# Which engine writes the halved high tiles: from VectorE to ScalarE, from unit 6 on

## The reference, cut to what matters

```
x = x + conv(group_norm(x), w0, b0)      # then the same with w1, b1
conv(f): fn = f / |f| over the channels
         vol = for each of the 5 x 5 shifts: sum over channels of fn * shifted fn     # 25 planes
         relu(w @ concat(f, vol) + b)                                                   # w is (512, 537)
```

## Time and profile before

| | us |
|---|---|
| median of 3 runs | 499.98 |
| lowest and highest | 497.35, 500.1 |
| profiled execution, its own time | 502.14 |
| its span in the trace | 500.4 |
| TensorE busy | 438.5 (88%) |
| VectorE busy | 370.1 (74%) |
| ScalarE busy | 288.1 (58%) |
| GpSimd busy | 119.1 (24%) |

### The profile page before, as it was taken

One profiled execution on the slowest core, in us unless ns is written; L12 is line 12 of the kernel. 1 busy time (PEld: TensorE's weight loads), 2 busy tenths in 40 slices (PEclk: granted clock), 3 DMA queues, 4 the chain that ended last, 5 costly groups with the idle time before them and its releaser, 6 DMA issues.

```text
span 500.4 us, 13879 instructions
## 1 busy us (share of the span) xinstructions
PE 438.5 (88%) x5896; PEld 225.3 (45%) x5896; DVE 370.1 (74%) x871; ACT 288.1 (58%) x346; POOL 119.1 (24%) x171
## 2 busy tenths in 40 slices
PE   0356599288699999999999999999999999999996
PEld 0342345153354545444444545454545454544442
DVE  6797797786777979597869797898879797533422
ACT  1454273647359585677757484849495857623222
POOL 3505340131111313105031313131313131143100
PEclk9968889879799999999999999999999999999999
DMA  8361351623131273526758684232222325355222
GB/s 298 127 220 51 99 193 57 180 55 74 45 94 32 66 227 99 162 106 208 267 172 260 225 258 131 63 83 67 73 78 61 90 78 156 149 170 177 104 118 92
DMA packets 33988, 65.87 MB, mean 132 GB/s; under 512 B 11756, under 2 KB 21028, under 8 KB 33926
## 3 DMA queue, kind: packets, MB, share of 16 engines
q1 hardware_dynamic: 24134, 56.07, 34.1%
q0 software_dynamic: 9792, 8.92, 7.5%
HBM read 33.54 MB, written 28.87 MB: 125 GB/s over the span
## 4 chain that ended last, share of the span: by engine, by line
PE 50%; DVE 21%; DMA 11%; ACT 10%; issue 4%; SPq 2%; POOL 2%; DVEq 0%; ACTq 0%
PE conv_ps L579 39%; DVE stats L820 7%; DVE operands L867 4%; ACT operands L685 4%; PE conv_ps L588 4%; PE gram_ps L501 3%; DMA skew<-band_dram 3%; DVE xs L952 3%; ACT v L692 3%; DMA band_dram<-band 3%; DMA vol<-corr_h 2%; PE gram_ps L514 2%; SPq L369 1%; ACT act_out L721 1%; POOL v L444 1%
## 5 line engine op out<-in xcount | busy, mean ns | idle before, releaser
L579 PE MATMUL conv_ps<-operands,wh 128*128 128x512 f16 x1024 | 327.8, 382 | 0.6 <-DVE wl L940 0.6
L579 PE MATMUL conv_ps<-operands,wl 128*128 128x512 f16 x512 | 195.4, 382 | 0.0
L579 PEld LDWEIGHTS conv_ps<-operands,wh 128*128 128x128 f16 x1024 | 101.7, 99 | 119.8 <-issue 3.5
L721 ACT ACTIVATE act_out<-conv_ps,bias,wdown 128x512 f32<-128x512 f32 x128 | 95.4, 771 | 86.4 <-PE conv_ps L588 84.0
L952 DVE TENSOR_TENSOR xs<-xs,act_out 128x512 f32<-128x512 f32 x128 | 85.7, 683 | 38.6 <-ACT act_out L721 38.6
L685 ACT ACTIVATE operands<-xs,affine 128x1024 f16<-128x1024 f32 x64 | 93.1, 1460 | 19.9 <-DVE affine L860 19.9
L867 DVE TENSOR_TENSOR operands<-v,operands 128x1024 f16<-128x1024 f32 x64 | 82.4, 1288 | 25.5 <-ACT v L692 19.8
L820 DVE BATCH_NORM_STATS2 stats<-xs 128x6 f32<-128x512 f32 x128 | 79.8, 681 | 2.5 <-DMA xs<-in_x_dram 2.5
L579 PEld LDWEIGHTS conv_ps<-operands,wl 128*128 128x128 f16 x512 | 50.4, 99 | 56.2 <-issue 1.6
L692 ACT ACTIVATE v<-xs,affine 128x1024 f32<-128x1024 f32 x52 | 68.5, 1317 | 0.0
L323 POOL DMA_DIRECT2D vol<-corr_h x48 | 33.1, 697 | 119.3 <-DVE corr_h L889 119.2
(11 more groups left out here) (75 smaller groups left out, 220.2 us busy)
## 6 DMA issues: line engine op xcount, KB each, us to landing
xs<-in_x_dram SPq DMA_DIRECT2D x32, 512.0 KB, 7.3
out_dram<-xs SPq DMA_DIRECT2D x32, 512.0 KB, 3.1
band_dram<-band SPq DMA_DIRECT2D x64, 120.0 KB, 2.6
skew<-band_dram SPq DMA_DIRECT2D x32, 222.5 KB, 3.1
vol<-corr_h POOLq DMA_DIRECT2D x48, 50.0 KB, 3.3
rows_dram<-rows SPq DMA_DIRECT2D x32, 65.8 KB
rows_dram<-rows SPq DMA_DIRECT2D x32, 63.3 KB
mirror<-rows_dram POOLq DMA_DIRECT2D x14, 110.9 KB, 2.5
```

Source lines behind the costliest of these rows:

```text
L579: pe.matmul(conv_ps[:, g % 4, :], w[:, l, t, m * P:(m + 1) * P], opnd[:, u % RING, part, t, n * HALF:(n + 1) * HALF], start=(t == 0 and w ...
L721: act.activation(in_rows(act_out[:, g % AOUT, :]), by_rows(conv_ps[:, g % 4, :]), ACT.Relu, bias=bias[:, l, m:m + 1], scale=wdown[:, l, m: ...
```

## The change

For units 6 to 15 ScalarE writes the halved tile, right behind the exact tile of the same t, and VectorE's half_tile returns at once. Units 0 to 5 are as before. The new function waits for the products of the unit before (which read half) and for its own high tile. The wait of TensorE on halved is not changed.

```
         def half_on_act(u):

             return u > STEADY + 2

@@ ScalarE
             def act_half_tile(u, t):

                 if half_on_act(u):
                     act.wait_ge(gram, BANKS * u)
                     act.wait_ge(high, KT * u + t + 1)
                     act.activation(half[:, t, :], opnd[:, u % RING, 0, t, :], ACT.Copy, scale=0.5
                                    ).then_inc(halved, 1)
...
                     norm_tile(k + 1, 0)
                     exact_tile(k + 1, 0)
+                    act_half_tile(k + 1, 0)
...
                     norm_tile(k + 1, 1)
                     exact_tile(k + 1, 1)
+                    act_half_tile(k + 1, 1)
...
                     if j in (1, 2) and valid(k + 1):
                         exact_tile(k + 1, j + 1)
+                        act_half_tile(k + 1, j + 1)
@@ VectorE
             def half_tile(u, t):

+                if half_on_act(u):
+                    return
                 wait(dve, gram, BANKS * u)
                 dve.tensor_scalar(half[:, t, :], opnd[:, u % RING, 0, t, :], 0.5, None, ALU.mult).then_inc(halved, 1)
```

## The result

The changed kernel takes **514.67 us** (median; 512.21 to 515.77), the kernel before 498.76 in the same comparison. The ratio is 1.029, with a 95% interval of 1.0251 to 1.0329: slower by 15.9 us from median to median. Two of the four runs of before took 497.35 and 497.55 us, the other two 499.98 and 500.1; in larger sets, on other chips, its medians are 499.94, 500.46 and 501.25, and 514.67 is 13.4 to 14.7 us above these. The profiled execution took 513.97 us, with a span of 512.1; that is 11.8 more than the profiled execution of before (502.14). The forecast was 513.7 and +13.75.

A forecast was written before the change was run, and what follows sets the result against it. TensorE's own work was taken to bound the kernel from slot 5 on, at 26.13 us a slot. Stalls in ten slots summed to 13.75 us, which on the median of 499.98 gave 513.7 us, range 507 to 524.

The forecast's parts named there:

- The bound: From slot 5 on TensorE's own work sets the pace, with a floor of 26.13 us a slot.
- The price of the copy: Each ScalarE copy of a halved tile lasts 1.05 us and moves what is queued behind it by 0.95 us.
- The stall: TensorE waits at step 6 for step 2's rectified group: 3.8 - 0.8 - 1.5 = 1.5 us in slot 12.
- Hole and slack: Slot 12: ScalarE idles 0.8 us before the lengths; step 2's rectified group is 1.5 us ahead of TensorE's need.
- A: Theory: an awaited rectified group stands behind ScalarE's copies; every slot pays 4 x 0.95 us less a hole and a slack.
- Nothing is taken back, nothing piles up: TensorE's 8.60 us of gapless work after step 6 recovers no stall; each slot pays anew, without accumulating lateness.
- The sum: Stalls of ten slots, 5 to 14: 6.0 + 1.5 + 2.4 + 1.1 + 1.3 + 1.45 = 13.75 us.
- (a): Rival: not slower, through larger slack or a copy under 0.57 us in slot 12; 498 to 500 us, chance 0.14.
- (b): Rival: copy near the exact tile's price, or late rows copy delays TensorE through the volume; 524 us, 0.10 with (c).
- (c): Rival: stalls lower TensorE's clock, costing 2 us more a slot; 534 us, chance 0.10 together with (b).

The follow-up runs named there:

- VectorE's relief alone: Against the kernel before: from unit 6 VectorE halves only 8 of 1024 columns per tile, products read the high tile, ScalarE unchanged; 499.99 us, ratio 1.0001.
- the later unit: Against the changed kernel: halved tiles move to ScalarE from unit 11 on in place of unit 6; 506.62 us, ratio 1.0129 to the kernel before.
- The other place: Against the changed kernel: same forty copies, tile 0 before the lengths, 1 behind the last exact tile, 2 and 3 behind the rows copy; 505.17 us.
- the two halves: Two kernels against the changed one: ScalarE halves only tiles 0 and 1, or only 2 and 3, VectorE the others; 504.55 and 508.41 us.
- the half length: Against the changed kernel: ScalarE writes columns 0 to 511 of each halved tile, VectorE the other 512; 502.1 us, ratio 1.0047 to the kernel before.
- the kernel with the copies alone: Against the changed kernel: VectorE halves all tiles again, ScalarE's forty copies go into a spare buffer nobody reads; 514.54 us, ratio 1.0306 to before.

## Why the prediction was right

**The bound.** Right. TensorE's 26.13 us a slot is a floor: the kernel with VectorE's relief alone has it in most slots, and in none of the eleven kernels is a slot from 5 on shorter by more than 0.02 us.

**The price of the copy.** Taken as 1.05 us and 0.95 in the queue, measured 1045 ns and 0.94. The value lies between the line through other forms (986 ns) and the weights' scaling (1104), as reasoned. The overlap was quoted as 0.10 from rows that give 0.13 (1.34 - 1.21); the copy's own is 0.09. The sentence on the Trainium skill ("ScalarE: Activation LUTs", "What ACT_TABLE_LOAD costs") gave 1039 ns; the trace agrees with it within 6 ns. The rule of the same page of the Trainium skill that sends multiplications to VectorE ("Rules for kernel authors") also holds here: 1045 ns against 444.

**The stall.** Hole and slack were read right, and the estimate of 0.1 us for the semaphore, which no row had been given for, is 0.07 (386.68 - 386.61). 3.8 - 0.8 - 1.5 = 1.5 us was forecast for slot 12 at step 6, and the group of step 6 starts 18.98 - 17.53 = 1.45 us later in its slot. Step 5 was to be 0.2 to 0.3 late and is 0.31. That a late volume or neighbour tile would be covered by this stall was right too: slot 8 has a wait of 0.6 us for the volume and is no longer than the others. The copies into a spare buffer and the later unit come out in A's ranges (the latter with a rise of 5.4 to 6.4 us where 7.6 was given). The other place, the two halves and the half length move as the order asks and not as the load does, but each ended 1 to 4 us over A's range. Two smaller readings were off. TensorE did wait for ScalarE once from 150 us on, 0.5 us at 164 us, ahead of the slots that count. And the list of waits was to show 1.5 us a slot; it shows 0.97.

**Nothing is taken back, nothing piles up.** Right: ten waits, nine nearly equal slots, and five waits when five slots are changed. That VectorE stays just ahead of the average was right as well, with 0.05 to 0.09 us to spare. In the kernel with tiles 0 and 1 moved VectorE was later, and did become the limit.

**The sum.** Here a term was mis-sized. Slots 6 and 7 were given 1.2 us and slot 8 1.1, on top of slots of 27.56, 27.14 and 27.28 us, with waits for the skew transfer, the neighbours and the statistics taken as part of the kernel. Measured from trace to trace these slots grow by 0.23, 0.56 and 0.41 only, slots 5 and 10 to 13 by 1.48 to 1.56, slot 9 by 1.21, and the nine sum to 10.0 us. The reason is that most of those waits did not come again. In slot 6 the lengths start 212.51 - 199.81 = 12.70 us behind the average in the trace, and 11.87 in the changed kernel, where ScalarE's chain alone puts them at 11.75. Had they been as late again, the slot of 28.20 us in the kernel with the copies alone suggests that it would have cost nearly as much more. Against typical slots of before, 236.1 us for nine, the change costs 1.43 a slot, 14.3 in ten; the rule of 1.5 in each of ten would have given 15.0.

So the way the total came out is in part luck. On its own base the sum made 515.9 us, 1.9 over the profiled execution. The same 13.75, lowered by waits of one trace, was then put on a median of executions that mostly don't have these waits, and that gave 513.7, 1.0 under the measured median. The rise from median to median, 15.9, is itself uncertain by some 2 us, as the medians of before show.

**The rivals.** (a) "Not slower" turned at 0.57 us a copy; the half-length copy, 0.51 in the queue, leaves slots 10 to 13 at 26.2 us, so the turn was priced right for slots like 12. It still costs 2.2 us in all, through slots 6 to 9, so a copy under the turn isn't quite free. (b) The copy was not near the exact tile's price, and the volume did not reach the time. (c) The clock stayed at 1.00.

## What to carry to other kernels

An engine that is busy 58% of the span can be full exactly where it matters. Before work is moved to it, read in one period which of its instructions is waited for next, and by how much it is ahead; work up to hole plus slack is free, and each microsecond over it cost a microsecond in every period here. Where a step must move, place it behind the instruction that others wait for, and look at the chain that comes next: here VectorE's statistics were within 0.1 us of being the limit. And when one trace shows waits of a few tenths in some periods only, take a second trace before they are entered in a sum, above all if that execution lies 2 us over the median.

## What the runs showed of the hardware

Waits of TensorE of 0.97 us, once in each slot, left the granted clock at 1.00. In the kernel with the copies placed elsewhere, TensorE stood still for 0.41 and 1.78 us within one slot, 10, for a reason that the profile doesn't name, and some 1.5 us after it went on its matmuls took 0.63 us again, the 1.2 GHz level. TensorE's rows there, and the stretch from the average on:

```profile
334.68 0.21 PE L505 MATMUL gram_ps<-operands 128*32 128x72 f16 x1 [1.78 <-issue]
...
335.08 0.38 PE L583 MATMUL conv_ps<-operands,wh 128*128 128x512 f16 x1
...
337.00 0.63 PE L583 MATMUL conv_ps<-operands,wl 128*128 128x512 f16 x1
```

```profile
334.83:339.00 4.17, 4.17 (x19) 1.78 (x15) 3.09 (x15) 2.28 (x4) 0.00 (x0) 0.66 0.36 87
```

That slot, 11, lasted 27.82 us with TensorE busy all of it, 1.7 over the floor. So these two stalls, 2.2 us together, were followed by a loss nearly as large, which the stalls of this change were not. It happened once, and what stopped TensorE stays open, as does whether the stalls alone brought the clock down. The page "TensorE: Matmul & The Clock Gate" of the Trainium skill, section "Part 1: The HAM clock gate (the "warmup" mystery)", says that an idle engine goes back to the lower level; the earlier trace rows agree (0.63 us a matmul right behind a wait of 6.21), and here the fall came when the engine was working again.
